# Two products of the expert stage rewritten: content from two half sums, and c2s in single passes behind one sum over experts

## The reference, cut to what matters

```python
spikes_enc = sigmoid(x @ enc_W + enc_b)                       # 256 -> 512
cont = spikes_enc @ s2c_W + s2c_b                             # 512 -> 64, "content"
gates = top-2 of 8, from tanh(cont @ rW1 + rb1) @ rW2 + rb2
h = relu(cont @ We1[e] + be1[e])                              # 64 -> 256, for each of 8 experts
output = sum over e of gates[e] * (h[e] @ We2[e] + be2[e])    # 256 -> 64
spikes_moe = sigmoid(output @ c2s_W + c2s_b)                  # 64 -> 512
decoded = sigmoid(spikes_moe @ dec_W + dec_b)                 # 512 -> 256, then a layer norm
```

## Time and profile before

| | us |
|---|---|
| three runs | 1729.6, 1735.58, 1733.74 (median 1733.74) |
| the profiled execution | 1731.6 |
| its span, first to last instruction | 1729.7 |
| PE busy in it | 1580.8 (91%) |
| DVE, ACT, POOL busy | 1282.3, 796.1, 142.4 |
| granted PE clock, mean | 0.981 of full speed |

### The profile page before, as it was taken

The page is one execution under the profiler, slowest core; times in us unless marked ns, Lnnn a source line. Parts: engine busy times, 40 slices in busy tenths (PEclk is TensorE's granted clock), DMA queues, the critical chain, the costliest instruction groups (busy, mean ns, idle before and its releaser), DMA issues. The chain is left out here.

```text
span 1729.7 us, 28622 instructions
## 1 busy us (share of the span) xinstructions
PE 1580.8 (91%) x10647; PEld 888.6 (51%) x10662; DVE 1282.3 (74%) x3200; ACT 796.1 (46%) x1509; POOL 142.4 (8%) x157
## 2 busy tenths in 40 slices
PE   6599899999999999999899999999999998897988
PEld 2163564445554465544655456444555446454546
DVE  6969857986589966798668885798657986755834
ACT  1133435445364543645355353544536454462555
POOL 1010110101101020000201001010110102000000
PEclk9899999999999999999999999999999999998999
DMA  9130440014300152011700225001530015205000
GB/s 332 57 129 1 160 148 2 16 74 166 93 3 16 74 189 70 3 51 45 236 15 2 87 85 174 2 16 74 179 80 3 15 74 187 62 3 147 3 13 13
DMA packets 50279, 133.99 MB, mean 77 GB/s; under 512 B 6272, under 2 KB 22592, under 8 KB 45536
## 3 DMA queue, kind: packets, MB, share of 16 engines
q1 hardware_dynamic: 50144, 132.16, 23.2%
HBM read 80.99 MB, written 46.04 MB: 73 GB/s over the span
## 5 line engine op out<-in xcount | busy, mean ns | idle before, releaser
L1360 DVE TENSOR_TENSOR arena_AB<-qT,kT 128x2048 f32<-128x2048 f32 (+3 forms) x240 | 401.7, 1716 | 10.9 <-PE bank L1691 5.1
L1417 DVE CUSTOM_DVE_ANT_0 bank<-bank,causal_b 128x512 f32<-128x512 f32 (+3 forms) x512 | 233.5, 526 | 122.3 <-PE bank L1763 121.8
L1609 PE MATMUL bank<-arena_F,kept 128*128 128x512 f32 (+1 forms) x528 | 233.6, 590 | 3.1 <-ACT arena_F L1109 1.2
L1691 PE MATMUL bank<-arena_AB,slot_w 128*32 128x512 f32 x1408 | 198.8, 609 | 37.0 <-DVE arena_AB L1360 36.8
L1184 ACT ACTIVATE arena_AB<-bank 128x512 f32<-128x512 f32 (+1 forms) x352 | 167.1, 583 | 93.0 <-PE bank L1779 93.0
L1219 ACT ACTIVATE arena_F<-bank,kept 128x512 f32<-128x512 f32 (+1 forms) x256 | 154.7, 680 | 47.9 <-PE bank L1609 45.3
L1609 PEld LDWEIGHTS bank<-arena_F,kept 128*128 128x128 f32 x528 | 99.6, 196 | 107.0 <-issue 93.3
L1609 PE MATMUL bank<-xnT,kept 128*128 128x512 f32 x256 | 118.6, 617 | 6.1 <-ACT xnT L1109 5.4
L1609 PE MATMUL bank<-cont_hi,by_cont 128*128 128x512 f32 (+3 forms) x289 | 118.5, 414 | 5.8 <-DVE arena_AB L1417 5.4
L1049 POOL TENSOR_TENSOR rstd_F<-var_eps_F,minus_half 128x4 f32<-128x4 f32 (+1 forms) x34 | 47.5, 1396 | 921.9 <-DVE var_eps_F L1288 921.9
L1887 PE MATMUL bank<-kept,arena_F 128*128 128x256 f32 x512 | 116.4, 381 | 1.9 <-ACT arena_F L1236 1.1
(11 more groups left out here) (200 smaller groups left out, 2356.8 us busy)
## 6 DMA issues: line engine op xcount, KB each, us to landing
arena_AB<-band SPq DMA_DIRECT2D x32, 1344.0 KB, 6.7
arena_AB<-stacks SPq DMA_DIRECT2D x64, 384.0 KB
stacks<-arena_AB SPq DMA_DIRECT2D x48, 256.0 KB, 2.8
band<-arena_AB SPq DMA_DIRECT2D x32, 328.0 KB, 3.1
stacks<-xnT SPq DMA_DIRECT2D x32, 256.0 KB, 2.5
band<-kT SPq DMA_DIRECT2D x4, 1352.0 KB, 21.2
stacks<-xn SPq DMA_DIRECT2D x16, 256.0 KB, 3.0
kept<-kept_pack SPq DMA_DIRECT2D x1, 3765.0 KB, 18.9
```

The source lines that it names most:

```text
L1360: ins = nc.vector.tensor_tensor(prod[SET_AT[i]][:, col:col + c, :], qT[:, hf, :].unsqueeze(1).broadcast_to([P, c, T]), k, ALU.mult)
L1417: ins = nc.vector.tensor_tensor_reduce(out=s, in0=s, in1=causal[:, (TT - 1 - i) * P:T], scale=-1.0, scalar=BIG, op0=ALU.add, op1=ALU.min, ...
L1609: ins = nc.tensor.matmul(out(ps), w, x, start=n == 0, stop=n == len(pairs) - 1)
L1691: ins = nc.tensor.matmul(ps[HS * col:HS * (col + 1), :], slot_w[:, slot(n), :], prod[SET_AT[i]][:, col, :], start=r == 0, stop=False, skip ...
```

## The change

Four things.
- cont. A new phase `halves` takes the four products of t_enc in column tiles of 64: the products over rows 0 and 1 of `s2c_w` go to partitions 0 to 63, those over 2 and 3 to 64 to 127. ACT copies the two half sums to `moe_t`. cont is then one full f32 product with `pair_sum`, a 128 x 128 matrix of ones where row and column agree modulo 64; it adds the halves and writes the sum twice.
- c2s. A new phase `both` multiplies `moe` with the same `pair_sum`. ACT copies the result, rounded, to `cont_hi`, DVE writes the difference to `cont_lo`, and each c2s chunk is then two single-pass products with `c2s_w`, which now stands in the setup's pack and is split as We1 is.
- Setup. `by_cont` grows by 512 columns to 2624, `pair_sum` is built by two DVE additions, and the tile of ones moves into the arena.
- The planner's table gets the new phases, some DMA durations change, and all offsets, TICK and DEPTH have new numbers (TICK 0.02 to 0.039, DEPTH 1.95 to 1.7).

```diff
@@ -35,11 +35,11 @@
     ("enc_w", KD * FF), ("enc_b", KF), ("s2c_w", KF * 2 * M), ("s2c_b", 1), ("rb1", 1), ("rw2", E),
-    ("be1", 2 * E), ("we2", E * 2 * M), ("be2", E // 2), ("c2s_w", FF), ("c2s_b", KF),
+    ("be1", 2 * E), ("we2", E * 2 * M), ("be2", E // 2), ("c2s_b", KF),
     ("dec_w", KF * D), ("dec_b", D), ("ln_g", D), ("ln_b", D), ("before", E * E),
 ]
 PACK_S = [("pair_sel", (E // 2) * P), ("slot_mask", 4 * HS), ("se", J), ("is_slot", NG * P), ("ahead", T), ("causal", T),
-          ("causal_T", P), ("we1", E * EH), ("rw1", M)]
+          ("causal_T", P), ("we1", E * EH), ("rw1", M), ("c2s_w", FF)]
 
@@ -53,7 +53,7 @@
-S_W = SETUP_W - E * EH - M
+S_W = SETUP_W - E * EH - M - FF
 
 
@@ -287,7 +287,8 @@
         p.put(("enc", m), ("PE", us(1.72, 0.05), *[("turn", k, "ACT") for k in range(KD)]), ("ACT", us(0.6, 0.16)))
-    p.put("cont", ("PE", us(3.43, 0.05), *[("enc", m, "ACT") for m in range(KF)]), ("ACT", us(1.15, 0.3)), ("DVE", us(0.6, 0.1)))
+    p.put("halves", ("PE", us(1.72, 0.05), *[("enc", m, "ACT") for m in range(KF)]), ("ACT", us(0.6, 0.16)))
+    p.put("cont", ("PE", us(0.86, 0.0), ("halves", "ACT")), ("ACT", us(1.15, 0.3)), ("DVE", us(0.6, 0.1)))
     p.put("rh", ("PE", us(0.46, 0.05), ("cont", "DVE")), ("ACT", us(0.6, 0.16)))
     p.put("lg", ("PE", us(1.0, 0.0), ("rh", "ACT")), ("DVE", us(2.93, 1.2)))
     for kind, n in EXPERTS:
@@ -310,7 +311,9 @@
     for m in range(KF):
-        p.put(("c2s", m), ("PE", us(0.86, 0.0), ("eo", E // 2 - 1, "DVE")), ("ACT", us(0.6, 0.16)))
+        if m == 0:
+            p.put("both", ("PE", us(0.86, 0.0), ("eo", E // 2 - 1, "DVE")), ("ACT", us(0.6, 0.16)), ("DVE", us(0.67, 0.1)))
+        p.put(("c2s", m), ("PE", us(0.46, 0.05), ("both", "DVE")), ("ACT", us(0.6, 0.16)))
     for i in tiles:
         p.put(("dec", i), ("PE", 1.72, *[("c2s", m, "ACT") for m in range(KF)]), ("DVE", 0.36))
@@ -364,28 +367,30 @@
 LOAD, CLOCK = 0.1, 1.0
-TICK, DEPTH = 0.02, 1.95
+TICK, DEPTH = 0.039, 1.7
 
...
-    ("F", "ACT"): {"hid": 4, "gb": 3.2},
-    ("F", "DVE"): {"xn": -1900, "cont": -1250, "gates": -760},
-    ("F", "PE"): {"turn": 960, "rh": 479, "hid": 478, "eo": 2100, "dec": 9870},
...
+    ("F", "ACT"): {"hid": 560},
+    ("F", "DVE"): {"ln_b": 1510, "both": 1080},
+    ("F", "PE"): {"halves": -170, "hid": 2070, "c2s": 70, "dec": 9230},
...
@@ -475,7 +480,7 @@
     if stage in ("F", "G", "H"):
-        reader = "DVE" if kind in ("lg", "eo", "dec") else "ACT"
+        reader = "DVE" if kind in ("lg", "eo", "dec", "both") else "ACT"
         return [phase], reader
@@ -514,7 +519,7 @@
     kind = phase[0] if isinstance(phase, tuple) else phase
-    return kind in ("prod", "PV", "eo") or u.stage == "A" and kind == "oT"
+    return kind in ("prod", "PV", "eo", "halves") or u.stage == "A" and kind == "oT"
 
@@ -636,7 +641,7 @@
 SLOTS_SETUP, TABLES_SETUP = 5, 11
-DVE_SETUP = 26
+DVE_SETUP = 28
@@ -658,7 +663,7 @@
         **NORM, "var_2": 1, "rstd_2": 1, "lgd_ready": 1, "gexp_ready": 1, "gates_ready": 1, "dect_ready": TT,
-        "moe_ready": 1, "cont_lo_ready": 1, "x_ready": 1, "dve_step": 19,
+        "moe_ready": 1, "moe_hi_ready": 1, "cont_lo_ready": 1, "x_ready": 1, "dve_step": 19,
     },
@@ -686,11 +691,13 @@
         cont_lo = sb("cont_lo", [P, T], fp32r)[:]
-        by_cont = sb("by_cont", [P, E * EH + M], fp32r)
+        by_cont = sb("by_cont", [P, E * EH + M + FF], fp32r)
         we1 = by_cont[:, 0:E * EH].rearrange("p (e n) -> p e n", e=E)
         rw1 = by_cont[:, E * EH:E * EH + M]
+        c2s_w = by_cont[:, E * EH + M:E * EH + M + FF]
         rh = sb("rh", [P, T])
         gT = sb("gT", [P, T], bf16)
+        pair_sum = sb("pair_sum", [P, P])
         V = sb("V", [P, TT, VW])
         V_b = sb("V_b", [P, TT, VW])
@@ -698,7 +705,6 @@
         minus_half = sb("minus_half", [P, TT])
-        ones = sb("ones", [P, P])
         half_c2s_b = sb("half_c2s_b", [P, KF])
@@ -784,6 +790,7 @@
         setup_only = arena["F"][:, 0:SETUP_W]
+        ones = arena["F"][:, ARENA["F"] - P:ARENA["F"]]
 
@@ -1202,6 +1209,10 @@
+                elif kind == "halves":
+                    act.wait_ge(*bank_full(u, "halves"))
+                    ps, read = place(u, "halves")
+                    nc.scalar.copy(moe_t[:, cols], ps[:, 0:w]).then_inc(read, 1)
                 elif kind == "cont":
@@ -1230,6 +1241,9 @@
+                elif kind == "both":
+                    act.wait_ge(*bank_full(u, name))
+                    nc.scalar.copy(cont_hi[:, cols], place(u, name)[0][:, 0:w]).then_inc(sem[u.stage]["moe_hi_ready"], 1)
                 elif kind == "c2s":
@@ -1519,6 +1533,11 @@
+                elif kind == "both":
+                    dve.wait_ge(*nth(u, "moe_hi_ready", 1))
+                    ps, read = place(u, name)
+                    nc.vector.tensor_tensor(cont_lo[:, cols], ps[:, 0:w], cont_hi[:, cols].bitcast(fp32), ALU.subtract
+                                            ).then_inc(read, 1)
                 elif kind == "dec":
@@ -1582,6 +1601,8 @@
                     once(nc.vector.tensor_tensor(by_cont[M:P, :], given[M:P, :], rounded[M:P, :], ALU.subtract))
+                    for half in range(2):
+                        once(nc.vector.tensor_tensor(pair_sum[:, half * M:(half + 1) * M], ident[:, 0:M], ident[:, M:P], ALU.add))
                 elif name == "biases":
                     dve.wait_ge(setup_pe, 2)
@@ -1833,9 +1854,18 @@
+                elif kind == "halves":
+                    for x in covered(u, name, [("enc", m) for m in range(KF)]):
+                        pe.wait_ge(*bank_read(u, x))
+                    pe.wait_ge(*bank_free(u, name))
+                    ps, full_ = place(u, name, full)
+                    for k in range(2):
+                        for half in range(2):
+                            ins = nc.tensor.matmul(ps[M * half:M * (half + 1), 0:width], s2c_w[:, 2 * half + k, 0:M],
+                                                   t_enc[:, 2 * half + k, cols], start=k == 0, stop=k == 1)
+                    ins.then_inc(full_, 1)
                 elif kind == "cont":
-                    product(u, name, lambda ps: ps[:, 0:width], [(s2c_w[:, k, :], t_enc[:, k, cols]) for k in range(KF)],
-                            read=[("enc", m) for m in range(KF)])
+                    product(u, name, lambda ps: ps[:, 0:width], [(pair_sum[:], moe_t[:, cols])], read=["halves"])
                 elif kind == "rh":
                     pe.wait_ge(*nth(u, "cont_lo_ready", 1))
@@ -1874,10 +1904,14 @@
+                elif kind == "both":
+                    pe.wait_ge(*nth(u, "moe_ready", 1))
+                    product(u, name, lambda ps: ps[:, 0:width], [(pair_sum[:], moe[:, cols])])
                 elif kind == "c2s":
                     if n == 0:
-                        pe.wait_ge(*nth(u, "moe_ready", 1))
-                    product(u, name, lambda ps: ps[:, 0:width], [(c("c2s_w", n * P, P), moe[:, cols])])
+                        pe.wait_ge(*bank_read(u, "both"))
+                    w = c2s_w[:, n * P:(n + 1) * P]
+                    product(u, name, lambda ps: ps[:, 0:width], [(w, cont_hi[:, cols]), (w, cont_lo[:, cols])])
                 else:
                     for x in covered(u, name, [("c2s", m) for m in range(KF)]):
```

More of the change, by code:

```diff
@@ L182, in local_phases @@
             p.put(("p", i), ("ACT", 0.68, ("tS", i, "DVE")))
-            p.put(("write", i), ("SP", 0.4, ("p", i, "ACT")), ("DMA", (2.3, 2.3, 6.3, 5.0)[i]))
+            p.put(("write", i), ("SP", 0.4, ("p", i, "ACT")), ("DMA", (2.3, 2.3, 8.0, 6.4)[i]))
             if i > 0:
@@ L187, in local_phases @@
                                         *([("pA", k - 2, 3, "PE")] if k >= 2 else []),
-                                        *([("pB", k - 2, 1, "PE")] if k >= 3 else [])), ("DMA", (6.6, 8.3, 6.0, 6.5)[k]))
+                                        *([("pB", k - 2, 1, "PE")] if k >= 3 else [])), ("DMA", (6.3, 8.2, 6.5, 8.5)[k]))
             p.put(("far", i), ("POOL", (0.62, 2.12, 2.12, 3.63)[i], ("p", i, "ACT"), ("shift", "DMA"),
@@ L366 @@
 LOAD, CLOCK = 0.1, 1.0
-TICK, DEPTH = 0.02, 1.95
+TICK, DEPTH = 0.039, 1.7
 PULL = {
[L370 to L373, removed]
-    ("F", "ACT"): {"hid": 4, "gb": 3.2},
-    ("F", "DVE"): {"xn": -1900, "cont": -1250, "gates": -760},
-    ("F", "PE"): {"turn": 960, "rh": 479, "hid": 478, "eo": 2100, "dec": 9870},
[L377 to L380, removed]
+    ("A", "ACT"): {"sT": -1240},
+    ("A", "DVE"): {"stats": 290, "prod": 350, "tS": -810, "far_den": -470, "pB": -2100, "pr": -1910},
+    ("A", "PE"): {"pA": 350, "pB": -1840},
+    ("B", "DVE"): {"qk": 2190, "lo": 1830, "S": 590},
+    ("B", "PE"): {"qk": 2930, "S": 3790, "mT": 210, "ST": 800, "on": -80, "oNT": 570, "pr": 710},
+    ("B", "SP"): {"stack": 440},
+    ("F", "ACT"): {"hid": 560},
+    ("F", "DVE"): {"ln_b": 1510, "both": 1080},
+    ("F", "PE"): {"halves": -170, "hid": 2070, "c2s": 70, "dec": 9230},
+    ("G", "ACT"): {"hid": 480},
+    ("G", "PE"): {"cont": 610, "dec": 780},
```

(4 more changed lines are left out.)

## The result

The changed kernel takes 1749.31 us in the median of five runs (1747.77 to 1753.0), the kernel before 1729.6 us beside it (1725.18 to 1735.58): a ratio of 1.0096, 95% interval 1.0073 to 1.0118. It is slower by 1%, where 1717 us and a gain of 1% were forecast, and lies outside the range.

What follows compares the result with a forecast made beforehand. PE's work was taken to set the pace nearly everywhere. PE work -19.6, waits +2.5, copies +1, and 0 for head, end and order gave -16 us from 1731.6; between 1715.6 and 1717.6 it said 1717, range 1702 to 1730.

Steps and rivals of the forecast that it cites:

- Steps 1 to 3: PE's products for cont and c2s: 0.69 and 0.73 us saved a call, 0.1 lost at new gaps; 19.6 us in all.
- Rival E: The change's products: 64-column halves run one after the other, or weight loads show; 1739 to 1742 us, chance 0.01.
- Step 4: Three added waits per expert call, together 3.3 us, mostly covered by other work: 2.5 us taken, at most 50.
- (a): Wait from halves by ACT's copy to cont: PE needs 0.8 us of other work a call.
- (b): Wait from both by ACT's copy and DVE's difference to c2s: 1.5 us a call.
- (c): Wait from c2s to dec: dec is ready about 1.0 us after PE has left c2s.
- Rival A: The three hand-overs of an expert call find no ready work, 60% uncovered: 1743 us, chance 0.07.
- rival B: Saved PE time turns to idle where DVE sets the pace: 1726 us, chance 0.13.
- Step 5: Two added ACT copies and a DVE difference per call delay work queued behind them: 1 us, 0 to 5.
- Step 8: New offsets and planner constants reorder every engine, moving only PE's idle time: 0 taken, 9 us either way.
- Rival D: The new order is worse by some 15 us: about 1732 us, no change, chance 0.09.
- C: The new order is better as well, PE's idle in the middle falling by a tenth: 1708 us, chance 0.20.

Runs made afterwards that it cites:

- old_order: The changed kernel with PE in the order of the kernel before, nothing put in the new gaps: 1.0238 of before, 1774.79 us.
- f_none: The changed kernel's order on every engine, with halves and both taken out and the old cont and c2s products: 1.034 of before, 1798.77 us.
- searched: The changed kernel with only other scheduler offsets and DEPTH, from a longer search of the build-time plan: 1.0003 of before, 1732.41 us.
- searched2: The changed kernel with scheduler offsets and planner constants from a still longer search: 0.9981 of before, 1732.58 us.
- searched2_warm: searched2 plus unread bf16 filler products in three kinds of planned PE gaps, 70% of each gap: 0.9921 of before, 1722.6 us.

## Why the prediction was wrong

- *What bounds it.* That PE sets the pace holds for its work. But the argument took the granted clock for a constant. It stood in the earlier trace rows (0.92, 0.99, 0.95) and was in no term.
- *Steps 1 to 3, the products* (forecast -19.6, bounds 16 to 22). The products are right, the total is small: work fell by 24.0, by 22.5 in old_order, both just beyond the bound of 22. By starts in after, halves take 377.22 to 379.09, 1.87 us as forecast; the products with `pair_sum` 1.06 and 0.96 (forecast 0.97):

```profile
377.22 1.94 PE L1864 MATMUL bank<-arena_F,kept 128*64 128x512 f32 x8
379.09 1.92 PE L1712 MATMUL bank<-arena_AB,slot_w 128*32 128x512 f32 x16
383.76 1.12 PE L1630 MATMUL bank<-arena_F,pair_sum 128*128 128x512 f32 x2
384.82 1.06 PE L1712 MATMUL bank<-arena_AB,slot_w 128*32 128x512 f32 x6
415.81 1.12 PE L1630 MATMUL bank<-arena_F,pair_sum 128*128 128x512 f32 x2
416.77 0.38 PE L1673 MATMUL bank<-kept,oN 128*128 128x128 f32 x2
```

and the c2s chunks 418.51 to 420.46, 1.95 as forecast. These make 2.93 and 2.91 for 3.53 and 3.65, 1.34 a call (forecast 1.3), or 20 us for 15 calls. The other 4 us of work are partly the two half calls, which the forecast left out; the rest isn't settled.
- *The loads of single-pass products are hidden*, as forecast; in the last c2s chunks of one call:

```profile
419.55 0.39 PE L1630 MATMUL bank<-cont_hi,by_cont 128*128 128x512 f32 x1
419.55 0.19 PEld L1630 LDWEIGHTS bank<-cont_lo,by_cont 128*128 128x128 f32 x1
419.78 0.39 PE L1630 MATMUL bank<-cont_lo,by_cont 128*128 128x512 f32 x1
```

A pitch of 0.23 us stands over a load of 0.19, all rows in use. Rival E is out.
- *Step 4, the hand-overs* (forecast 2.5 of at most 50 us). The total for open gaps came near by luck: 53.3 us for 50. (a) is 0.73 us a call for 0.8, (b) 2.4 for 1.5, and (c), forecast at 1.0, showed no wait. In after they are covered, as forecast: PE's waits for cont_lo (L1512) are 1.3 us, and none for L1215, L1246 or L1539 has a place among its largest. Rival A is not what happened, though its 1743 us lies nearest to the time; nor is rival B, since the wait for products grew by 2.7 us only. But the step priced the cover at nothing, and the cover is the order's: in before's order it isn't there.
- *Step 5, the copies* (forecast 0.6, 0.6 and 0.69 us each). The durations are right; the 1 us for what is queued behind them shows in no row by itself:

```profile
L1539 DVE TENSOR_TENSOR cont_lo<-bank,cont_hi 128x512 fp32r<-128x512 f32 x15 | 10.3, 686 | 5.9 <-ACT cont_hi L1246 5.9
L1246 ACT CAST cont_hi<-bank 128x512 fp32r<-128x512 f32 x15 | 8.9, 595 | 15.9 <-PE bank L1630 15.9
L1215 ACT COPY arena_F<-bank 128x512 f32<-128x512 f32 x15 | 8.8, 587 | 42.6 <-PE bank L1864 42.6
```

- *Step 6, the head.* The split and the sums end at 93.3 and DVE then waits 4.73 us for PE (7.09 in the earlier trace rows): hidden, as forecast. PE's busy time in the head is 2.7 us longer at a clock of 0.87 for 0.92, which is the clock again.
- *Step 7, the end.* From the first product of c2s to dec, 1731.44 to 1735.50, 4.06 us for 3.56 in the earlier trace rows: 0.5 more, where 0.35 was forecast.
- *Step 8, the offsets anew* (0, from -9 to +9). **This step failed.** The two crossed kernels bracket it: the change in the old order costs 42.3 us, the new order without the change 68.6, both together 21.1. Two effects that add would give 42.3 + 68.6. So the order can't be priced by itself, as the step did, nor at a tenth of the idle. Its premise, that a new order can only move PE's idle time, is wrong too: f_none has the products of before and 30.9 us more clock cost. The steps that were summed, 1 to 7, come to -16; what happened is 37 us above that by the profiled spans (+21.1). searched shows that it is the order and not the code: nearly all of it goes with nothing else changed (ratio 1.0096 to 1.0003, spans 1750.8 to 1730.1). In after, the order's price shows as idle at waits that the expert calls have no part in (oN, 4.2 to 13.9 us, and the score maxima, 10.4 to 21.4), as the prediction's last part had it, and as half clock behind them.
- *The missing term, the clock.* It is 33.0 us of PE's time in this sum. That it is 33 us of the kernel's time is not shown: 31.1 us less of it came with a gain of none to 10 us (1.0096 to 1.0068), and in the two better orders the filler returned 0.5 and 0.6% (1.0003 to 0.9953, 0.9981 to 0.9921). The filler takes PE time itself, so what the clock alone is worth to the kernel stays open.

Which single pull makes DVE close the expert call ahead of oN was not tried. Rival D named the right cause, but at 15 us, no change from before, and a chance of 0.09. C and D were taken as wings about a step worth zero, and no row bore out the zero.

## What to carry to other kernels

When an order fixed at build time is made anew with a change, split the two before any sum is believed: the new work in the old order, and the old work in the new one. Here both were slower than either whole kernel, and one more search of the order was worth 16 us where the edit saves 24 us of work. Take the granted clock as a term of its own (busy time times one less the clock, summed over short stretches). Before counting it as loss, test with filler products whether the kernel gets faster, and look whether the filler runs into real work.

## What the hardware showed

- A gap of 2.03 us on PE, with 0.6 and 0.5 us of short products about it, was followed by some 12 us at 1.2 GHz, through stretches in which PE was busy all the time (652 to 656). A gap of 0.60 us at the same place was not.
- Filler of 115 recorded products (their loads are recorded 123 times), 28.1 us of PE's busy time, came with 91 us less time at half clock, searched2 to searched2_warm:

```profile
L1960 PE MATMUL bank<-ahead,ident_b 128*128 128x512 bf16 x115 | 28.1, 379 | 7.9 <-DVE arena_AB L1445 7.5
```

- Less clock cost on PE, bought with filler, is not as much less kernel time: 31.1 us of it came with a gain of none to 10 us in one order, 38.8 us with 10 us of median in another.
- A hand-over that nothing covers holds PE for 0.73 us by way of one ACT copy, and for 2.4 us on average by way of an ACT copy and a DVE difference (old_order, 17 cases each).
